# Inverse scales of a cross-attention and quantised feed-forward block split by bit fields, with part of the work reordered between VectorE and GpSimd

## What is computed

```python
def bit_linear(x, w, b):
    gamma_x = clip(max(abs(x), axis=-1), 1e-05)
    scale_x = 127.0 / gamma_x
    x_dq = clip(round(x * scale_x), -128, 127) / scale_x
    gamma_w = clip(mean(abs(w)), 1e-05)
    w_dq = clip(round(w / gamma_w), -1, 1) * gamma_w
    return x_dq @ w_dq.T + b

q = ctx @ Wq.T + bq;  k = ctx @ Wk.T + bk
att = softmax(q @ k.T)
x = x + layernorm(x) @ att.T          # for each of the four batches
h = layernorm(x)
x = x + bit_linear(silu(bit_linear(h, gate_w, gate_b)) * bit_linear(h, val_w, val_b), out_w, out_b)
```

## Time and profile before

| | |
|---|---|
| median of three runs | 61.09 us |
| the profiled execution: its time | 60.99 us |
| its span, first to last instruction | 59.3 us |
| PE busy | 51.3 us (87%) |
| DVE busy | 48.2 us (81%) |
| ACT busy | 47.6 us (80%) |
| POOL busy | 44.9 us (76%) |
| granted TensorE clock | 1.0 |

### The profile page before, as it was taken

The page is one execution under the profiler, slowest core; times in us unless marked ns, Lnnn a source line. Parts: engine busy times, 40 slices in busy tenths (PEclk is TensorE's granted clock), DMA queues, the critical chain, the costliest instruction groups (busy, mean ns, idle before and its releaser), DMA issues.

```text
span 59.3 us, 1140 instructions
## 1 busy us (share of the span) xinstructions
PE 51.3 (87%) x298; PEld 32.7 (55%) x301; DVE 48.2 (81%) x122; ACT 47.6 (80%) x84; POOL 44.9 (76%) x102
## 2 busy tenths in 40 slices
PE   1999998899999699929899988899999997979910
PEld 1768866468888478613323634333473752759800
DVE  3249859897999799996998989898999997997150
ACT  0723929989999999979999685999999999798700
POOL 4970002798789888798779978989999999999900
DMA  0789999999993000000002001299270199920573
GB/s 0 161 232 369 409 339 409 408 407 411 397 400 136 0 17 0 0 6 0 6 0 44 0 0 32 57 180 174 51 137 0 31 185 178 242 72 0 176 235 120
DMA packets 11070, 8.92 MB, mean 150 GB/s; under 512 B 7605, under 2 KB 9141, under 8 KB 11065
## 3 DMA queue, kind: packets, MB, share of 16 engines
q1 hardware_dynamic: 10912, 8.72, 47.5%
q10 hardware_dynamic: 152, 0.14, 1.3%
HBM read 6.04 MB, written 1.05 MB: 120 GB/s over the span
## 4 chain that ended last, share of the span: by engine, by line
POOL 30%; PE 26%; issue 17%; DVE 12%; ACT 9%; POOLq 0%; ACTq 0%
POOL h L344 6%; PE psO L940 5%; PE psT L753 5%; POOL r_cols L276 4%; PE psV L763 3%; DVE nmax L467 3%; PE psG L763 3%; PE psH L940 3%; PE psT L778 3%; POOL rstd L311 3%; ACT o_early L723 3%; DVE x L485 3%; POOL pgam L325 2%; POOL res L372 2%; POOL w_int L409 2%
## 5 line engine op out<-in xcount | busy, mean ns | idle before, releaser
L572 DVE TENSOR_REDUCE pmax<-prod 128x1 f32<-128x1024 f32 x8 | 9.7, 1210 | 0.1
L707 ACT ACTIVATE sil<-psG,s_gv 128x1024 f32<-128x1024 f32 x8 | 8.9, 1112 | 0.6 <-PE psG L874 0.2
L556 DVE TENSOR_TENSOR prod<-psV,sil 128x1024 f32<-128x1024 f32 x7 | 8.5, 1221 | 0.9 <-ACT sil L707 0.5
L859 PE MATMUL psG<-ter_gate,hT 128*128 128x512 bf16 x31 | 8.0, 378 | 0.8 <-ACT sil L707 0.7
L886 PE MATMUL psV<-ter_val,hT 128*128 128x512 bf16 x26 | 7.0, 381 | 0.2 <-issue 0.2
L940 PE MATMUL psO<-ter_out,pT 128*128 128x256 bf16 x48 | 6.2, 273 | 0.7 <-ACT o_early L723 0.7
L940 PEld LDWEIGHTS psO<-ter_out,pT 128*128 128x128 bf16 x48 | 4.4, 98 | 2.4 <-DVE pT L599 0.8
L281 POOL TENSOR_SCALAR ve<-mv 128x2 f32<-128x2 f32 (+1 forms) x3 | 0.6, 197 | 6.0 <-DVE mv L463 5.9
L694 ACT ACTIVATE hT<-psH,unshift 128x256 bf16<-128x256 f16 x8 | 3.8, 475 | 1.5 <-PE psH L842 1.4
L859 PEld LDWEIGHTS psG<-ter_gate,hT 128*128 128x128 bf16 x32 | 2.7, 96 | 4.0 <-issue 2.0
L644 ACT ACTIVATE prob<-psT,nmax 128x256 f32<-128x256 f32 x8 | 3.7, 479 | 1.1 <-DVE nmax L467 1.1
(11 more groups left out here) (142 smaller groups left out, 144.9 us busy)
## 6 DMA issues: line engine op xcount, KB each, us to landing
w_gate<-in_w_gate SPq DMA_DIRECT2D x2, 512.0 KB, 5.1
x<-in_x_tok SPq DMA_DIRECT2D x4, 256.0 KB, 6.3
w_val<-in_w_val SPq DMA_DIRECT2D x2, 512.0 KB, 7.2
xt_sb<-in_x_T SPq DMA_DIRECT2D x4, 256.0 KB, 7.8
w_out<-in_w_out SPq DMA_DIRECT2D x2, 512.0 KB, 8.9
out_x<-res SPq DMA_DIRECT2D x8, 128.0 KB, 1.8
ctx_sb<-in_ctx_T SPq DMA_DIRECT2D x2, 128.0 KB, 2.8
ctx_sb<-in_ctx_T SPq DMA_DIRECT2D x1, 256.0 KB, 6.0
```

Source lines behind the costliest of these rows:

```text
L556: nc.vector.tensor_tensor(prod[:, t % P_RING, :], psV[:], sil[:, t % S_RING, :], ALU.mult).then_inc(prod_done, 1)
L572: nc.vector.tensor_reduce(pmax[:, t:t + 1], prod[:, t % P_RING, :], AX.X, ALU.max, apply_absolute_value=True).then_inc(pmax_done, 1)
L707: nc.scalar.activation(sil[:, t % S_RING, :], psG[:], ACT.Silu, scale=s_gv[:, t, 0:1]).then_inc(sil_done, 1)
L859: nc.tensor.matmul(psG[:, c * HC:(c + 1) * HC], hT[:, t, k, :], w_ter[0][:, k * HID + c * HC:k * HID + (c + 1) * HC], start=(k == 0), stop ...
```

## The change

Three things are done.

1. **The split.** `r_gv` gets a last axis of three. The upper 16 bits of a float32 are its bf16 truncation, and the view `r_top` reads them in place. So the parts need two subtractions (whole minus top, rest minus top) and then copies of the upper halves into `r_cols`: on POOL two copies (one for each value of q), each with its semaphore step, on DVE one copy. `gmin` becomes a function of its own, `smallest_p`, with its own semaphore.
2. **The first group's split is on DVE**, right behind `scales_h(0)`. The other two stay on POOL.
3. **New orders.** POOL makes `gamma_h(1)` before it rounds, rounds tiles 0, 1 and 2 in a row, then splits group 1, and it centres tiles 6 and 7, which ACT did. DVE has `h_inv(1)` and `scales_h(1)` early, before the sums `add_x(4)` to `add_x(7)`; the two clips of the value weights stand among these sums; `h_max(2)` stands behind `times_value(0)`.

```diff
-        r_gv = sb("r_gv", [P, T, 2])
-        r_rest = sb("r_rest", [P, T, 2, 2 * NPART])
+        r_gv = sb("r_gv", [P, T, 2, NPART])
...
+        r_top = r_gv[:].bitcast(BF16).rearrange("p t w (i two) -> p t w i two", two=2)[:, :, :, :, 1]
...
-                cols = r_cols[:, a:e, :].rearrange("p t (w q c) -> p t w q c", w=2, c=32)
-                whole = r_gv[:, a:e, :].unsqueeze(3).to_broadcast([P, e - a, 2, 2 * NPART])
-                rest = r_rest[:, a:e]
-                part = [cols[:, :, :, :, i:KB:NPART] for i in range(NPART)]
-                same(part[0], whole).then_inc(r_step[g], 1)
-                pool.wait_ge(r_step[g], 1)
-                nc.gpsimd.tensor_tensor(rest, whole, part[0], ALU.subtract).then_inc(r_step[g], 1)
-                pool.wait_ge(r_step[g], 2)
-                same(part[1], rest).then_inc(r_step[g], 1)
-                pool.wait_ge(r_step[g], 3)
-                nc.gpsimd.tensor_tensor(rest, rest, part[1], ALU.subtract).then_inc(r_step[g], 1)
-                pool.wait_ge(r_step[g], 4)
-                same(part[2], rest).then_inc(r_step[g], 1)
-                nc.gpsimd.tensor_scalar(gmin[:, a:e], r_gv[:, a:e, 1], -GAMMA_MIN, 1.0 / QMAX, ALU.mult,
-                                        ALU.mult).then_inc(r_step[g], 1)
+                for i in range(NPART - 1):
+                    if i:
+                        pool.wait_ge(r_step[g], i)
+                    nc.gpsimd.tensor_tensor(r_gv[:, a:e, :, i + 1], r_gv[:, a:e, :, i], r_top[:, a:e, :, i],
+                                            ALU.subtract).then_inc(r_step[g], 1)
+                pool.wait_ge(r_step[g], NPART - 1)
+                cols = r_cols[:, a:e, :].rearrange("p t (w q c) -> p (t w) q c", w=2, c=32)[:, :, :, 0:KB]
+                top = r_top[:, a:e].rearrange("p t w i -> p (t w) i").unsqueeze(2)
+                for q in range(2):
+                    same(cols[:, :, q, :].rearrange("p n (j i) -> p n j i", i=NPART),
+                         top.to_broadcast([P, 2 * (e - a), NPART, NPART])).then_inc(r_step[g], 1)
+
+            def smallest_p(g):
+
+                a, e = GROUPS[g]
+                pool.wait_ge(rgv_done, g + 1)
+                nc.gpsimd.tensor_scalar(gmin[:, a:e], r_gv[:, a:e, 1, 0], -GAMMA_MIN, 1.0 / QMAX, ALU.mult,
+                                        ALU.mult).then_inc(gmin_done, 1)
...
+            def inverse_parts(g):
+
+                a, e = GROUPS[g]
+                dve.wait_ge(rgv_done, g + 1)
+                dve.wait_ge(c_fill, 5)
+                for i in range(NPART - 1):
+                    if i:
+                        dve.wait_ge(r_step[g], i)
+                    nc.vector.tensor_tensor(r_gv[:, a:e, :, i + 1], r_gv[:, a:e, :, i], r_top[:, a:e, :, i],
+                                            ALU.subtract).then_inc(r_step[g], 1)
+                dve.wait_ge(r_step[g], NPART - 1)
+                cols = r_cols[:, a:e, :].rearrange("p t (w q c) -> p (t w) q c", w=2, c=32)[:, :, :, 0:KB]
+                top = r_top[:, a:e].rearrange("p t w i -> p (t w) i").unsqueeze(2).unsqueeze(3)
+                nc.vector.tensor_copy(cols.rearrange("p n q (j i) -> p n q j i", i=NPART),
+                                      top.to_broadcast([P, 2 * (e - a), 2, NPART, NPART])).then_inc(r_step[g], 2)
...
-            h_copy(0); centre_x2(5); h_copy(1); centre_x2(6); centre_x2(7); silu(0); abs_sum(2, 0); h_copy(2);
+            h_copy(0); centre_x2(5); h_copy(1); silu(0); abs_sum(2, 0); h_copy(2); silu(1); abs_sum(2, 1);
```

More of the change, by code:

```diff
@@ L177, in xattn_ffn @@
         r_step = [sem(f"r_step{g}") for g in range(len(GROUPS))]
+        gmin_done = sem("gmin_done")
         hT_ps = sem("hT_ps")
@@ L323, in gamma_p @@
                 pool.wait_ge(pmax_done, t + 1)
-                pool.wait_ge(r_step[group[t]], 6)
+                pool.wait_ge(gmin_done, group[t] + 1)
                 nc.gpsimd.tensor_scalar(pgam[:, t:t + 1], pmax[:, t:t + 1], 1.0 / QMAX, gmin[:, t:t + 1],
@@ L420, in _ @@
             add_bias(1); centre_x2(0); centre_x2(1); std_x2(0); std_x2(1); h_step(0); gamma_h(0); h_step(1);
[L421 to L428, removed]
+            gamma_h(1); h_round(0); h_round(1); h_round(2); inverse_parts(1); smallest_p(0); smallest_p(1);
+            centre_x2(4); h_round(3); centre_x2(6); centre_x2(7); std_x2(2); add_bias(2); h_step(2); gamma_h(2);
+            h_round(4); h_round(5); gamma_p(0); h_round(6); inverse_parts(2); smallest_p(2); gamma_p(1);
+            p_round_int(0); add_bias(3); gamma_p(2); h_round(7); to_int(2, 0); to_int(2, 1); gamma_p(3);
+            shift_x(); add_bias(4); scale_out(0); add_bias_shift(5); gamma_p(4); p_round_int(3); scale_out(1);
+            add_residual(0); scale_out(2); add_bias_shift(6); scale_out(3); gamma_p(6); add_residual(1);
+            p_round(6); add_bias_shift(7); scale_out(4); scale_out(5); add_residual(2); add_residual(3);
+            add_residual(4); scale_out(6); scale_out(7)
         @block.vector
@@ L531, in scales_h @@
                 dve.wait_ge(sgv_done, g + 1)
-                nc.vector.reciprocal(r_gv[:, a:e, :], s_gv[:, a:e, :]).then_inc(rgv_done, 1)
+                nc.vector.reciprocal(r_gv[:, a:e, :, 0], s_gv[:, a:e, :]).then_inc(rgv_done, 1)
+            def inverse_parts(g):
[12 more added lines that the diff above has]
+                                      top.to_broadcast([P, 2 * (e - a), 2, NPART, NPART])).then_inc(r_step[g], 2)
             def gamma_w(w):
@@ L577, in gamma_p @@
                 dve.wait_ge(pmax_done, t + 1)
-                dve.wait_ge(r_step[group[t]], 6)
+                dve.wait_ge(gmin_done, group[t] + 1)
                 nc.vector.tensor_scalar(pgam[:, t:t + 1], pmax[:, t:t + 1], 1.0 / QMAX, gmin[:, t:t + 1],
@@ L612, in _ @@
             mean_x2(2); stats_x2(3); gamma_w(1); mean_x2(3); centre_x2(2); h_max(0); h_max(1); scales_w(1);
[L613 to L621 removed]
+            h_inv(0); h_inv(1); scales_h(0); inverse_parts(0); scales_h(1); add_x(4); add_x(5); clip(0, 1);
+            stats_x2(4); stats_x2(5); mean_x2(4); mean_x2(5); clip(1, 0); add_x(6); clip(1, 1); add_x(7);
+            stats_x2(6); stats_x2(7); mean_x2(6); mean_x2(7); times_value(0); h_max(2); p_max(0); h_inv(2);
+            times_value(1); scales_h(2); p_max(1); times_value(2); invert_gamma_p(0); p_max(2);
+            invert_gamma_p(1); gamma_w(2); times_value(3); scales_w(2); invert_gamma_p(2); p_max(3);
+            times_value(4); clip(2, 0); clip(2, 1); p_max(4); times_value(5); invert_gamma_p(3); p_max(5);
+            invert_gamma_p(4); widen(2); gamma_p(5); invert_gamma_p(5); times_value(6); p_max(6); widen(3);
+            invert_gamma_p(6); times_value_half(0); times_value_half(1); p_max(7); gamma_p(7);
+            invert_gamma_p(7); p_round_half(1); p_copy(6); add_residual(5); add_residual(6); add_residual(7)
         @block.scalar
```

38 lines of the change are left out of this document (15 added, 23 removed).

## The result

The changed kernel takes 61.25 us (median of 11 runs, 61.08 to 61.83) against 60.81 us for the kernel before (11 runs, 60.56 to 61.53). The ratio is 1.0084, with a 95% interval from 1.0053 to 1.0115: slower by some 0.5 us. The change is inside 1%, as the likeliest case had it, and it lies on the other side of no change than the sum said (-0.1 us). Measured once more beside an experiment further down, the ratio was 1.0106 (1.0054 to 1.0157).

What follows compares the result with a forecast made beforehand. A relay of waits over all engines, not one engine's sum, was taken as the bound. The profiled 60.99 us less 0.09 at the fifth product gave 60.9, with 0.10 for the runs' median 61.0 us; range 60.4 to 61.8.

Steps and rivals of the forecast that it cites:

- the likeliest case: Whole kernel: the time stays within 1% (about 0.61 us) of the kernel before; chance 0.66.
- the sum: Whole kernel: all terms together, 0.09 us earlier at the fifth product, end time 61.0 us.
- the relay: Steady state: a product ends, PE adds the next tile's bias and value product, the next product starts; 2.74 us a step.
- Tile 0's chain: POOL, PE and ACT ahead of silu(0): 0.33 us earlier, 0.2 from the roundings and 0.13 from the first group's r_cols.
- ACT without its centrings: ACT loses two centrings (0.90 us) ahead of silu(0), which only PE then limits: start 27.56, end 28.66.
- VectorE's list up to the first product: DVE: with the split put in, add_x(4) starts 1.22 us later, yet DVE is free at about 28.4, before silu(0) ends.
- the cover of 0.26: DVE ahead of the first product: 0.26 us of slack left between its list and the end of silu(0).
- The maximum moved: DVE between first and second product: first 0.59 us earlier at 28.66, second at 32.15, 0.17 later than before.
- rival B: POOL late with group 2's step: its 0.3 us of cover goes and the second product is held; 61.3 us, chance 0.12.
- rivals C: The gain is kept: the first product's 0.59 us arrives at the end; 60.5 us, chance 0.15.
- Rival A: DVE's split stalls behind GpSimd's roundings: first product 0.5 to 0.9 us later, 61.4 to 61.9 us; chance 0.25.
- Its second part: DVE's clips of the value weights, beside POOL's centring of tile 4 and rounding of tile 3, could add 0.4 us.

Runs made afterwards that it cites:

- e2: The changed kernel with group 0's split back on POOL, between the roundings of tiles 0 and 1; ratio to the kernel before 1.0005.
- e1: The kernel before with only the new split, on POOL for all groups, all orders as before; ratio to the kernel before 0.9956, measured again 0.9952.
- e3: The changed kernel with POOL's rounding of tile 0 waiting until DVE has finished group 0's split; ratio to the kernel before 1.0056.
- e5: e1 with DVE's maximum of tiles 4 to 7 moved behind the first product; ratio to the kernel before 0.9998.
- e8: e1 with group 0's split on DVE, right behind its scales, other orders as before; ratio to the kernel before 1.0099.
- e4: e1 with the centring of tile 7 moved from ACT to POOL; ratio to the kernel before 0.9957.
- e6: e4 with group 1's scales on DVE moved to behind add_x(5), POOL's gamma_h(1) and rounding of tile 1 early; ratio to the kernel before 0.9992.

## Why the prediction was right or wrong

**What bounds the kernel, and the relay: right.** From the second product on the steps were 2.73, 2.75 and 2.75. Each product began 0.10 or 0.11 us after PE's last matmul into its bank; the silus had ended 0.8, 0.2 and 0.3 us before.

**Tile 0's chain, 0.33 earlier: right in size, wrong in what it needs.** At silu(0) e2 has 0.31 of it and e1 0.29. But the prediction got it from POOL being rid of the split, and saw the earlier `r_cols` as an extra. e1, with the split on POOL and all old orders, shows that 0.29 comes from the new split's shorter form alone.

**ACT without its centrings: silu(0) by PE alone, right only without the DVE split.** In e2 silu(0) waits for PE, as named, and the first product is 0.05 from its place. In the changed kernel ACT waited 1.00 us for a mean from DVE. The centring of tile 5 stayed in ACT's queue, and I had moved DVE's list by 1.22 without asking who waits for its means. Two of POOL's three waits are of that kind as well.

**VectorE's list up to the first product: this is the step that failed.** I gave the two subtractions a distance of 0.20 each and the copy 0.14. With POOL idle that is right: e3 has 1.09 us from the reciprocal to the first sum, and my numbers make 1.04. Beside the roundings it is 1.59. The 0.50 of waiting, the 0.05 by which e3 exceeds my sum, 0.13 in the rest of the list (4.34 from the first sum to the product, where the prediction's 24.19 and 28.4 make 4.21) and 0.02 at its head, less the cover of 0.26, are the 0.44 by which the first product was late (8.42 against 7.98). What had been weighed wrongly is the evidence in the earlier trace rows: a cast that took 0.24 us longer beside a cast of POOL's. I set against it an `s_gv` that ran beside a POOL instruction at no cost. But that instruction took 0.23 us in all and was over at 22.86, `s_gv` at 22.84: to wait for its end would have cost 0.03 us, which one row cannot tell from nothing. The Trainium skill ("SBUF — State Buffer", section "SBUF: two separate sides") has the rule, an exclusive lock between GpSimd and a VectorE instruction in a fast mode or with two SBUF inputs, the latter only against a GpSimd instruction that reads SBUF. On two inputs the runs agree with it: the subtractions took 0.68 and 0.49 us beside reading, 0.37 beside memsets. The copy has one input and was held beside memsets too, which the part on a fast mode would explain; no run shows the mode that it ran in.

**The maximum moved: right.** 3.48 in e2, e3 and e5. In the changed kernel it was 3.59: the reciprocal of group 2's step came at 32.41, right behind POOL's step (32.12 and 0.26 long), some 0.10 late against e2. That is rival B in small: its cover of 0.3 was used up because the means that POOL waits for were late.

**Sum.** The second product was to be 0.17 late and was 0.71. 0.44 of the difference is the first product's, 0.10 the wait of the reciprocal. The fifth was to be 0.09 early and was 0.46 late, the same difference of 0.55. (The range's ends, 60.4 and 61.8, are 0.1 below what rivals C and A had worked out, 60.5 and 61.9; nothing hangs on it.)

**Rival A** named place and cause, and nearly the size: the first product came 0.44 later than forecast, where it had 0.5 to 0.9, and the fifth 0.55, where it had 0.4 to 0.8 at the end. Its second part did not come: the 0.4 that the clips might add on DVE fell on POOL instead. It had a chance of 0.25 against the forecast's 0.48, and the only row against it could not carry that.

**What the change consists of,** by the fifth product: new split -0.29 (e1), maximum behind the product +0.25 (e5 against e1), all other orders -0.03 (e2 against e5), group 0's split on DVE +0.53 (changed against e2). These are the steps from one kernel to the next, so they add up to the 0.46 seen by construction; in another order they would differ, as e8 shows, where the same split costs 0.81. Of the 0.53, e3 gives back 0.38 by keeping POOL still. The other 0.15 need not be the price of the work: silu(0), which holds the first product in e2 and in e3, ends 0.14 later in e3 (8.14 against 8.00), and e3's DVE was free before either time, at 7.96. Waiting for GpSimd is thus between 0.38 and all of it.

## What to carry to other kernels

A list of tiny instructions has no price of its own: look at what runs beside each on the neighbour that can hold it up, and charge what is left of *that* instruction. When an edit bundles a cheaper form with new orders, time the form alone with the old orders first; here the form was all of the gain. And before you move work to an engine because a neighbour is the busy one, list who waits for the results that stand behind it in the queue.

## What the runs showed of the hardware that was not expected

- A VectorE instruction on 4 or 8 elements per partition takes up to 0.48 us beside a 256-element GpSimd instruction, against 0.15 to 0.2 alone, and ends 0.01 us behind it (0.43 for the second subtraction, 0.33 for `s_gv` in e2, 0.35 in e4, 0.48 in e1).
- What is left of a held instruction when GpSimd's ends is less than its time alone by 0.13 to 0.16 us, an estimate from three kinds: 0.01 of 0.17 for a subtraction, 0.06 of 0.21 for the copy, 0.28 of 0.41 for the cast of the earlier trace rows.
- Only reading holds the two-operand subtraction: 0.37 us for two beside memsets and beside nothing, 0.49 beside GpSimd instructions that read. The 72-element bf16 copy is stretched by both (0.29 and 0.32 against 0.21).
- It works the other way too: GpSimd's 0.48 us centring takes 0.68 to 0.80 beside VectorE's clips (changed kernel, e4, e6).
- On GpSimd the whole split is 1.15 us now (in e1 two subtractions from 23.68, copies done at 24.83), where the old form took 1.64 to the end of its last copy (23.28 to 24.92).
